# First node pass of a graph network kernel: x through a ring of four tiles instead of eight, loops over four groups instead of eight

## The reference, cut to what matters

```python
h = jnp.maximum(_layernorm(x, axis=-1), 0.0)
x = x + _L0_gnn_ref(src, dst, h, L0_gnn_W, L0_gnn_b)   # (h @ W + b) scaled by degree, messages over edges
h = jnp.maximum(_layernorm(x, axis=-1), 0.0)
x = x + _L1_gnn_ref(h, edge_index, ...)                # edge messages, polynomial, batch statistics
```

## Time and profile before

| What | us |
|---|---|
| median of three runs | 2392.77 |
| the profiled execution's own time | 2393.98 |
| its span, first to last instruction | 2391.9 |
| first node pass, first statistics to last | 141 to 897 |
| of it, ten bodies of eight steps in the loops | 272 to 852 |

### The profile page before, as it was taken

How to read it: one execution, slowest core, us unless ns; L and a number is a source line. 1 busy time by engine, 2 the same in 40 slices (tenths; PEclk the granted TensorE clock), 3 DMA queues, 4 the chain that set the end, 5 groups by cost and what they waited for, 6 DMA issues and landing times.

```text
span 2391.9 us, 53054 instructions
## 1 busy us (share of the span) xinstructions
PE 1860.9 (78%) x13930; PEld 1471.4 (62%) x13930; DVE 1820.3 (76%) x8033; ACT 1542.4 (64%) x3485; POOL 1181.8 (49%) x1159
## 2 busy tenths in 40 slices
PE   6968999999998978888857777759999677777200
PEld 4645776677776756555646666647777677777200
DVE  6766887888897865555538888959998799999653
ACT  4746777777787754444436666648887799999100
POOL 2125554555554536777747777753331121211575
PEclk9978999999999989999979999979999899999655
DMA  5673444444443434555436666656665688888775
GB/s 174 240 171 98 149 148 138 141 152 149 141 158 132 152 101 68 80 80 81 80 57 116 120 119 121 113 134 195 195 194 187 205 287 289 288 288 280 236 243 173
DMA packets 195484, 387.11 MB, mean 162 GB/s; under 512 B 50096, under 2 KB 88781, under 8 KB 195366
## 3 DMA queue, kind: packets, MB, share of 16 engines
q1 hardware_dynamic: 122678, 310.43, 38.3%
q0 software_dynamic: 59584, 74.91, 17.2%
q10 hardware_dynamic: 13104, 0.61, 0.6%
HBM read 194.86 MB, written 193.49 MB: 162 GB/s over the span
## 4 chain that ended last, share of the span: by engine, by line
PE 33%; issue 20%; DVE 14%; POOL 12%; ACT 11%; DMA 5%; SPq 2%; another core or an unknown queue 2%; DVEq 0%; ACTq 0%; POOLq 0%
PE bank L755 9%; ACT hb L1007 6%; POOL big L483 5%; PE bank L729 5%; POOL x_tab L494 4%; PE bank L775 3%; DVE x1b L1337 2%; PE bank L860 2%; POOL msg_tab L494 2%; PE bank L884 2%; PE bank L718 2%; DVE st L1351 2%; PE bank L873 2%; ACT ht L1143 2%; PE bank L885 2%
## 5 line engine op out<-in xcount | busy, mean ns | idle before, releaser
L755 PE MATMUL bank<-w_sb,ht 128*128 128x256 f32 x1568 | 405.8, 402 | 6.6 <-issue 6.5
L1259 DVE BATCH_NORM_STATS2 st<-big 128x6 f32<-128x256 f32 x686 | 247.2, 416 | 208.1 <-DMA big<-in_x_dram,idx 125.2
L755 PEld LDWEIGHTS bank<-w_sb,ht 128*128 128x128 f32 x1568 | 291.2, 196 | 87.5 <-issue 54.2
L729 PE MATMUL bank<-ident,hb 128*128 128x128 f32 x1568 | 213.9, 279 | 105.0 <-ACT hb L1007 74.8
L483 POOL DMA_INDIRECT big<-x_tab,idx x196 | 192.2, 981 | 183.6 <-ACT h L1007 126.2
L729 PEld LDWEIGHTS bank<-ident,hb 128*128 128x128 f32 x1568 | 176.2, 142 | 141.5 <-issue 100.4
L462 POOL DMA_INDIRECT node_edge<-node_tab,idx x196 | 188.2, 960 | 134.7 <-DVE x1b L1337 85.9
L973 ACT ACTIVATE h2b<-x1b,rs 128x256 f32<-128x256 f32 x392 | 214.4, 597 | 37.1 <-remote 28.6
L538 POOL TENSOR_TENSOR big<-big,bias 128x256 f32<-128x256 f32 x98 | 71.7, 731 | 329.9 <-ACT hb L1007 283.6
L968 ACT ACTIVATE hb<-big,rs 128x256 f32<-128x256 f32 x392 | 211.8, 589 | 12.5 <-DVE rs L1282 11.3
L1007 ACT ACTIVATE hb<-big,rs 128x256 f32<-128x256 f32 x392 | 213.3, 591 | 1.4 <-DVE rs L1282 1.4
(11 more groups left out here) (242 smaller groups left out, 4725.1 us busy)
## 6 DMA issues: line engine op xcount, KB each, us to landing
big<-in_x_dram SPq DMA_DIRECT2D x97, 512.0 KB
x_tab<-x1b SPq DMA_DIRECT2D x97, 512.0 KB
big<-x_tab SPq DMA_DIRECT2D x97, 512.0 KB
out_dram<-x1b SPq DMA_DIRECT2D x97, 512.0 KB, 2.9
msg_tab<-zeros SPq DMA_DIRECT2D x50, 256.0 KB, 2.2
tpw_tab<-tpb SPq DMA_DIRECT2D x49, 256.0 KB, 2.0
tpb<-tpw_tab SPq DMA_DIRECT2D x49, 256.0 KB
big<-msg_tab SPq DMA_DIRECT2D x49, 256.0 KB
```

The lines of the kernel that those rows point to most:

```text
L729: last = nc.tensor.transpose(bank[q][:, (2 * j + k) * P:(2 * j + k + 1) * P], hb[:, s.slot(2, 2), 2 * q + j, k * P:(k + 1) * P], ident[:])
L755: last = mm(y, ht[:, q, (2 * j + k) * P:(2 * j + k + 1) * P], w_sb[:, k, :], start=False, stop=(j == 1 and k == 1))
L1259: last = v.bn_stats(st[:, k, j, :], row)
```

## The change

- The first pass loads x through four slots of `big` instead of eight: group s goes to slot s mod 4, and its load waits that `x1` of group s-4 is done, not s-8.
- All four engines with a loop in the first pass (SyncE, TensorE, ScalarE, VectorE) run it with `run`: two bodies of four steps written out, then a loop of 22 bodies of four steps in place of 11 bodies of eight. As many steps as before (8 at the beginning, those from 96 on at the end) are written out.
- The semaphores of the loads are four instead of eight; the second node pass adds four of its own for its slots 4 to 7. The second node pass itself keeps its ring and its loops.

```diff
+X1 = 4
...
-        x_in, x1_out, ... = (sems("x_in", XS), sems("x1_out", 2), ...
+        x_in, x1_out, ... = (sems("x_in", X1), sems("x1_out", 2), ...
...
-        y_in, y_out = reused(x_in, G, XS), sems("y_out", 2)
+        y_in, y_out = reused(x_in, G, X1) + sems("y_in", XS - X1), sems("y_out", 2)
...
             def p1_step(s):                                  # SyncE
                 if s.live():
-                    done(sp, p1["x1"], s, XS, per=2)
+                    done(sp, p1["x1"], s, X1, per=2)
                     rows, n = group(x_groups, s)
-                    sp.dma_start(big[0:n, s.slot(0, XS), 0:J * D], rows).then_inc(x_in[s.slot(0, XS)].sem, 16)
+                    sp.dma_start(big[0:n, s.slot(0, X1), 0:J * D], rows).then_inc(x_in[s.slot(0, X1)].sem, 16)
                 if s.live(4):
                     done(sp, p1["x1"], s, 4, per=2)
...
-            run_groups(sp, 4, p1_step)
+            run(sp, G, 4, p1_step)
...
-            run_groups(pe, 5, p1_step)
+            run(pe, G, 5, p1_step)
...
-            run_groups(act, 4, p1_step)
+            run(act, G, 4, p1_step)
...
-            run_groups(dve, 3, p1_step)
+            run(dve, G, 3, p1_step)
```

More of the change, by code:

```diff
@@ L350, in build @@
                          "relu2 gram")
-        x_in, x1_out, claim_out, node_in, win_in = (sems("x_in", XS), sems("x1_out", 2), sems("claim_out", 1), sems("node_in", 1),
+        x_in, x1_out, claim_out, node_in, win_in = (sems("x_in", X1), sems("x1_out", 2), sems("claim_out", 1), sems("node_in", 1),
                                                    sems("win_in", 1))
@@ L967, in relu1 @@
                     a = s.slot(1, 2)
-                    return s_act(hb[:, a, j, :], xj(big, s.slot(1, XS), D)[:, j, :], ACT.Relu,
+                    return s_act(hb[:, a, j, :], xj(big, s.slot(1, X1), D)[:, j, :], ACT.Relu,
                                  bias=rs[:, 0, a, 1, j:j + 1], scale=rs[:, 0, a, 0, j:j + 1])
@@ L1290, in own_moments @@
                     for j in js:
-                        last = v.bn_stats(st[:, 0, j, :], xj(big, s.slot(0, XS), D)[:, j, :])
+                        last = v.bn_stats(st[:, 0, j, :], xj(big, s.slot(0, X1), D)[:, j, :])
                     return last
@@ L1332, in p1_step @@
                             j = 2 * q + i
-                            y, row = bank[2 + q][:, i * D:(i + 1) * D], xj(big, s.slot(2, XS), D)[:, j, :]
+                            y, row = bank[2 + q][:, i * D:(i + 1) * D], xj(big, s.slot(2, X1), D)[:, j, :]
                             weight = dinv2[:, bass.ds(s.at(2) * J + j, 1)]
```

## The result

The changed kernel takes 2409.47 us (median of 9 runs, 2403.86 to 2420.87) against 2392.77 us. The ratio is 1.0068, with a 95% interval of 1.0049 to 1.0087: 0.7% slower, by 16.7 us between the medians, where 16 us less were forecast. The time lies above the forecast's range.

The account below looks back on a forecast made before the run. It took TensorE and VectorE together to pace the first pass. Pauses gone gave 22.0 us less 5.9 us of waits, 16.1 us, other terms nothing: 2394.0 to 2377.9 us, median 2377, range 2364 to 2402.

Parts of the forecast that it names:

- Short loops end the pauses: First pass, VectorE's loop: bodies of four steps remove ten pauses at backward branches, 19.0 us, 22.0 us at most with L1335.
- The reading of "issue" at L1291 as an instruction fetch: VectorE's idle time before the statistics of x is a code fetch at each backward branch, 1.9 us each, 19.0 in all.
- The size of that gain: First pass: ending VectorE's pauses gains 16.1 us, 22.0 us less 5.9 us given back in waits for TensorE.
- TensorE's end (10): Low end of the gain, 10 us: TensorE strictly paces the first pass, so only its own idle time is won.
- VectorE's (22): High end of the gain, 22 us: VectorE strictly paces the first pass, so all its pauses are won.
- an ordinary step carries 0.585 us of waiting: VectorE at L1335: each step without a pause waits 0.585 us for TensorE, so ten steps give back 5.9 us.
- TensorE is late next: First pass: with VectorE's pauses gone TensorE is the next limit, so the gain lies between 10 and 22 us.
- TensorE paces the stage: Rival, first pass: pauses only hid TensorE's deficit, gain 4 to 10 us; chance 0.34 together with small clock losses.
- the load now goes first and needs less ... I cost it at nothing: SyncE's ring of four: the load, later but ahead of the store, has at least 3.7 us to spare; cost nothing.
- GpSimd's queue waits for x1 alone: Premise of the ring's zero cost: GpSimd's queue depends only on x1 and so follows the pass.
- the prediction had every stage keep its length: Stages after the first pass keep their code and lengths and simply move up with it; cost nothing.
- pauses that might stay: Rival, VectorE's loop: all 21 branches of the shorter body pause 1.9 us, +20.9 us, 2414; chance 0.09.

Follow-up runs that it names:

- series C: Follow-up runs on another chip, without slow spells: load order alone, load lateness alone, Gram products left out; the kernel before took 2283.8 us.
- series D: Follow-up runs on another chip, without slow spells: the changed kernel again beside variants of it; the kernel before took 2281.0 us.
- store_first_loops8: Changed kernel with SyncE's store ahead of the load and all loops back at eight steps; ratio 1.0002 to the kernel before.
- series B: Follow-up runs with slow spells: four variants of the changed kernel, with loops back at eight steps or the store first; the kernel before took 2375 us.
- series A: The result itself, with slow spells, chip not known: changed kernel 2409.47 us against 2392.77 us for the kernel before, ratio 1.0068.
- store_first: Changed kernel with SyncE issuing the store of x1 ahead of the load of x; ratio to the kernel before 1.0034, repeated without spells 0.9936.
- ring4_loops8: Changed kernel (ring of four, load first) with all four loops back at eight steps; ratio 1.0112 to the kernel before.
- E: Follow-up runs with slow spells: changed kernel again (1.0080), fewer Gram products, extra TensorE products; the kernel before took 2396.0 us.
- F: Follow-up runs on another chip, without slow spells, repeating load order alone and lateness alone; the kernel before took 2282.1 us.
- nogram_before_again: Kernel before without 15 of 16 Gram products per step in the first pass, repeated with slow spells; ratio 0.9806 to the kernel before.
- ring8_load_first: Kernel before with one edit: SyncE issues the load ahead of the store, as early as before; ratio 1.0062 to the kernel before.
- ring8_load_first_again: Repeat, on another chip, of the kernel before with the load issued ahead of the store, no later; ratio 1.0077 to the kernel before.
- nogram_before: Kernel before without 15 of 16 Gram products per step in the first pass, in a series without spells; ratio 1.0000 to the kernel before.
- after_again: The changed kernel run once more, in a series without slow spells; ratio 0.9937 to the kernel before, 13.3 us faster.
- nogram_after: Changed kernel without 15 of 16 Gram products per step in the first pass; ratio 0.9861 to the kernel before, repeated 0.9860.
- ring8_late: Kernel before with one edit: the load goes out one step later, still behind the store; ratio 0.9996 to the kernel before.

## Why the prediction was wrong

**Short loops end the pauses: right.** 19.0 us at the statistics of x became 0.0, 49 instruction packets became 3, TensorE's idle time before its transposes fell from 12.8 to 5.9 us (7.6 to 0 without spells). The reading of "issue" at L1291 as an instruction fetch holds: where the fetch's packet landed 1.46 us later (series C), the pause was 1.38 us longer.

**The size of that gain: a little high.** I forecast 16.1 us, between TensorE's end (10) and VectorE's (22). Where it can be seen, in series D, the change as a whole gained 13.3 us, and the 80 steps 10.3. The ordinary step there shows no wait for TensorE at L1335 (3.7 us in all in store_first_loops8, all of it "issue"); the pause is won until TensorE's 6.44 us a step are reached, and no further. The term "an ordinary step carries 0.585 us of waiting" was taken from a trace in which that wait was made by spells.

**"TensorE is late next": right as a direction, wrong in its strength.** The rival "TensorE paces the stage" named the place where the gain goes, L1335, and priced it at a remaining gain of 4 to 10 us. In series B the loops made no difference (1.0112, 1.0116, 1.0124), so with spells and the load first the gain is nothing. What I took for an ordinary deficit of TensorE was largely 53 instructions that started 0.46 to 1.31 us behind the one before them in the kernel before's own trace. The earlier trace rows had the sign of it: 10.9 us of idle time labelled "issue" before L718 and 6.5 before L755, in places where nothing is waited for. I used neither number.

**The step that failed: "the load now goes first and needs less ... I cost it at nothing".** It asked only whether the data come in time. They do: with the load late the ratio is 0.9996 and 1.0001 without spells, and in the loops of the changed kernel L1292 never waited for a DMA. It did not ask what the two transfers meet on their way. Put back into its old order, the changed kernel is at 1.0034 with spells, where its three variants with the load first are at 1.011 to 1.012. In the kernel before's own structure, the order alone costs 0.62 and 0.77%, by pauses 1.4 us longer and the clock behind them; that way is closed to the changed kernel, which has no pauses, and without spells it indeed pays nothing (0.9937 and 0.9936). With spells the traces point at a slower TensorE, and there the way is not shown: the half-speed clock covered 37 to 58 us of the 80 steps in the three kernels with the load first and 20 us with the store first, and slow instructions were 42 to 55 against 52, so the clock moved with it and the spells' number did not. The premise beside it, that "GpSimd's queue waits for x1 alone", was wrong too: its scatters waited 26.9 us for each other's landing before and 50.8 us after, though series D shows no cost of that.

**The sum for the measured series** can't be closed. By series B, the forecast's -16.1 became 0, the order added 0.8%, near 19 us, and store_first's 0.34%, 8 us, is left over. I don't know what that is: short loops, late loads and the slots are together in it, and the two runs that should have split it came in a series without spells. These 8 us and the 19 us are more than the 16.7 us measured in series A, where the kernel before had another time than in series B (2393 against 2375). And some 5 us of the loss in A lie behind the pass, where the prediction had every stage keep its length.

**The forecast's signs.** "TensorE paces" would be shown by a wait at L1335 up by 12 us or more; it rose by 24.4. The high end, 2402, was set by pauses that might stay, not by transfers that meet each other, and was 7.5 us short.

**Better than both?** Without spells store_first is as fast as the changed kernel (2266.0 against 2267.8 us in series D), and with them 0.8% faster than ring4_loops8 (series B). It still loses 0.34% to the kernel before in series B. Neither version beats the kernel before everywhere; where both orders were measured, the store first was never the slower one.

## What to carry to other kernels

When a change moves a DMA command past another one, price what the two meet, not only whether the data are in time: in series C the packet of an instruction fetch took 1.36 us behind a 512 KB load and 0.56 us behind a store. An idle time labelled "issue" in the middle of a run of matmuls is a finding of its own; as long as it is unexplained, a gain on another engine that has to pass through TensorE should be given a good chance of nothing. And compare within one series of runs, and on more than one chip: the kernel before differed by 5% between series, and with it the sign of this change. Last, before an experiment is said to have ended something, count over the whole stage and by a second sign: here the count began at 205 us and saw starts alone, and it missed slowness both before 205 us and in the ends.

## What the runs showed of the hardware that I had not expected

- TensorE can have spells in which it starts an instruction only each 0.7 us, in the middle of a product and with no wait: series A, B and E, in the first pass. In series C, D and F there were none, in the same kernels. A series with spells is 91 to 115 us slower for the kernel before. Most of it is lost in this pass: of 114 us between the profiled executions of the kernel before and of store_first_loops8, 34 us in the first 14 groups, 53 us in the 80 steps and 12 us in the last steps. Both series B and E ran on one chip, and C, D and F on three others. Their cause is open. TensorE's modelled ends can hide it: 10 us at 190 us in nogram_before_again.
- The clock fell behind spells (51 of 52 half-speed stretches) and behind VectorE's pauses, which leave TensorE idle for some 2 us (four, six and five stretches in ring8_load_first, ring8_load_first_again and nogram_before), and not by how busy TensorE was: granted clock 1.00 with TensorE busy 480 of 480 us (after_again) and with 442.12 of 480 (nogram_after), against 0.97 with 430.63 of 480 (nogram_before):

```profile
272.00:752.00 480.00, 430.63 (x2025) 303.71 (x2022) 441.56 (x2094) 405.89 (x869) 288.99 (x298) 0.97 0.47 159
```

- A loop body of 233 VectorE instructions fetches its code anew in each turn, at 1.9 us of idle time; one of 116 doesn't, in 21 turns. At that branch an 8 KB instruction packet took 0.56 us in the mean behind a store to memory (ring8_late) and 1.36 us behind a load from it (ring8_load_first).
